# Scales stored as 16 rows, and a rewritten first stretch, in a LayerNorm + S4 + int4 SwiGLU kernel

## What is computed

```
xn = layernorm(u)                                   # over the 1024 channels, no weights
K  = S4 convolution kernel of length 1024 (64 states, from Lambda, p, q, Vc, Ct, B, step)
y1 = irfft(rfft(xn, 2048) * rfft(K, 2048))[..., :1024] + D * xn
Wg, Wu [2752, 1024], Wd [1024, 2752] = (int4 word - zero) * scale, one scale and zero per 64 inputs
h  = silu(xn @ Wg.T) * (xn @ Wu.T)
out = u + y1 + h @ Wd.T
```

## Time and profile before

| | |
|---|---|
| runs (median, lowest to highest) | 1475.91 us, 1475.70 to 1476.86, n = 3 |
| profiled execution | 1472.47 us, span 1470.6 us |
| mean granted TensorE clock | 0.968 |
| busy: TensorE matmul | 1337.2 us, 91% |
| busy: VectorE, GpSimd, ScalarE | 962.1, 678.0, 462.3 us |
| unit 0, unit 2, unit 4 and the down projection begin | 70.7, 164.4, 211.9, about 1001 us |

### The profile page before, as it was taken

One profiled execution on the slowest core, in us unless ns is written; L12 is line 12 of the kernel. 1 busy time (PEld: TensorE's weight loads), 2 busy tenths in 40 slices (PEclk: granted clock), 3 DMA queues, 4 the chain that ended last, 5 costly groups with the idle time before them and its releaser, 6 DMA issues.

```text
span 1470.6 us, 17062 instructions
## 1 busy us (share of the span) xinstructions
PE 1337.2 (91%) x6301; PEld 632.9 (43%) x6301; DVE 962.1 (65%) x1038; ACT 462.3 (31%) x825; POOL 678.0 (46%) x483
## 2 busy tenths in 40 slices
PE   1557798999999999999999999778999999999998
PEld 1533343444443444444444444333454444444444
DVE  3854478999989898999898988624243341432341
ACT  2643335454444544544444444221000000000000
POOL 3643458777777686787979797430000000000000
PEclk9877999999999999999999999998999999999999
DMA  6301144444444444454444443599636336335331
GB/s 178 89 29 70 38 136 148 153 131 165 138 161 147 161 139 154 132 170 139 164 141 165 141 146 120 190 406 316 229 97 224 109 105 213 108 106 197 125 94 57
DMA packets 164358, 218.09 MB, mean 148 GB/s; under 512 B 41394, under 2 KB 121908, under 8 KB 162356
## 3 DMA queue, kind: packets, MB, share of 16 engines
q1 hardware_dynamic: 163412, 202.78, 42.5%
q10 hardware_dynamic: 864, 14.22, 2.3%
HBM read 139.64 MB, written 77.34 MB: 148 GB/s over the span
## 4 chain that ended last, share of the span: by engine, by line
PE 39%; DVE 5%; DMA 4%; POOL 4%; SPq 2%; issue 2%; ACT 1%; ACTq 0%; DVEq 0%
PE px L1381 15%; PE pz L1381 8%; PE pv L1408 5%; PE px L1293 4%; PE py L1381 4%; DMA sz<-in_sz_up 2%; PE pz L1293 2%; POOL wo L660 2%; DVE wf L1466 1%; POOL hs L679 1%; DMA kshift<-kpad 1%; DMA w_d<-ds 1%; POOL ds L669 1%; DVE wf L1464 1%; SPq L568 1%
## 5 line engine op out<-in xcount | busy, mean ns | idle before, releaser
L1293 PE MATMUL px<-xo,wo 128*128 128x512 f16 x2016 | 477.0, 391 | 31.9 <-ACT u L936 19.3
L1293 PEld LDWEIGHTS px<-xo,wo 128*128 128x128 f16 x2016 | 200.7, 101 | 284.4 <-issue 43.5
L660 POOL TENSOR_TENSOR wo<-wf,wo 128x512 f16<-128x512 f32 x147 | 233.5, 1598 | 85.1 <-ACT wo L882 84.7
L679 POOL TENSOR_TENSOR hs<-hf,hs 128x512 f16<-128x512 f32 x154 | 212.3, 1384 | 118.0 <-ACT hs L917 117.8
L1293 PE MATMUL pz<-xo,wo 128*128 128x512 f16 x1008 | 232.6, 381 | 0.0
L1381 PE MATMUL px<-wd,hr 128*128 128x512 f16 x1056 | 232.3, 379 | 0.0
L1381 PEld LDWEIGHTS px<-wd,hr 128*128 128x128 f16 x1056 | 102.2, 98 | 118.7
L1293 PEld LDWEIGHTS pz<-xo,wo 128*128 128x128 f16 x1008 | 99.0, 98 | 119.3 <-issue 2.2
L917 ACT ACTIVATE hs<-hf 128x512 f16<-128x512 f32 x154 | 94.4, 621 | 90.7 <-DVE hf L1556 45.1
L1913 DVE SCALAR_TENSOR_TENSOR acc<-px,acc 128x512 f32<-128x512 f32 x32 | 22.1, 691 | 153.0 <-PE px L1381 125.5
L669 POOL TENSOR_TENSOR ds<-wf,ds 128x512 f16<-128x512 f32 x73 | 113.0, 1547 | 10.8 <-ACT ds L903 10.8
(11 more groups left out here) (217 smaller groups left out, 1417.3 us busy)
## 6 DMA issues: line engine op xcount, KB each, us to landing
h_d<-hs SPq DMA_DIRECT2D x154, 256.0 KB, 4.6
hr<-h_d SPq DMA_DIRECT2D x56, 704.0 KB, 4.3
w_d<-ds SPq DMA_DIRECT2D x73, 256.0 KB, 3.9
wd<-w_d ACTq DMA_DIRECT2D x4, 2816.0 KB, 15.2
sz<-in_sz_gate SPq DMA_DIRECT2D x21, 512.0 KB
sz<-in_sz_up SPq DMA_DIRECT2D x21, 512.0 KB
sz<-in_sz_down SPq DMA_DIRECT2D x20, 512.0 KB
xc_d<-xo SPq DMA_DIRECT2D x8, 1024.0 KB, 10.9
```

Of the source, the lines that this page charges most:

```text
L660: pool.tensor_tensor(w_dest(t, j, 1), w_place_of(j), w_dest(t, j, 0), ALU.subtract).then_inc(wlo_done, 1)
L679: pool.tensor_tensor(hs[:, j, :, 1, :], h_place_of(p, j), hs[:, j, :, 0, :], ALU.subtract)\
L1293: done = pe.matmul(bank[:, :], wo[t % 2][:, j, wp, k * P:(k + 1) * P], xo[p][:, j, xp, k, :], start=(j in (0, 3) and k == 0 and wp == 0 an ...
```

## The change

Two parts.

**Scales.** The host repeats the rows, so that a slab's scales have 16 rows, each read by 8 partitions. The bytes that reach SBUF are the same. In the short slabs the source has one row for 2 partitions in place of one for 32.

**Head.** The 28 transposes of the first half go round all eight banks, those of the second half round five, two or five (HEAD_BANK). The order of the seven blocks of a group is A11, A12, A22, S1, S3, S2, S4 (X_ORDER). All eight groups have buffers of their own, so no load of a group waits; sum S3 overwrites block A21 in place, and the second half has two sets of three sum buffers. SyncE loads all eight groups before the slabs of tile 1. Behind the products of units 0 and 1 stand 2, 3, 1, 1, 1, 1, 3 and 1, 1, 1, 1, 1, 1, 10 transposes (BESIDE). The lists of VectorE, ScalarE and GpSimd until unit 2 are written anew.

```
--- before.py
+++ after.py
+X_ORDER = (A11, A12, A22, S1, S3, S2, S4)
+HEAD_BANK = [("v0", "v1", "x1", "y1", "z1", "x0", "y0", "z0")[(n + 1) % 8] for n in range(28)] + \
+            ["v0", "v1", "x1", "y1", "z1"] * 2 + ["v0", "v1"] * 2 + \
+            ["v0", "v1", "y0", "z0", "x0"] * 2 + ["v0", "v1"] * 2
+def head_bank_free(n):
+    return max([m + 1 for m in range(n) if HEAD_BANK[m] == HEAD_BANK[n]], default=0)
...
+BESIDE = [(28, 30), (30, 33), (33, 34), (34, 35), (35, 36), (36, 37), (37, 40),
+          (40, 41), (41, 42), (42, 43), (43, 44), (44, 45), (45, 46), (46, 56)]
...
-        sum_first = [at(f"xs{q}", [P, 4, SB], f32, X0 + (88 + 8 * q) * K1) for q in range(3)]
-        x_second = [at(f"xb{q}", [P, 2, H], f32, H0 + (20 + 8 * q) * K1) for q in range(2)]
+        sum_first = [at(f"xs{q}", [P, 3, SB], f32, X0 + (88 + 6 * q) * K1) for q in range(4)]
+        x_second = [at(f"xb{q}", [P, 2, H], f32, (H0 + 12 * K1, H0 + 28 * K1, H0 + 20 * K1, W0 + 8 * K1)[q]) for q in range(4)]
...
             def load_x(q):
                 b = 8 * (q // 4) + q % 4
-                if q >= 6:
-                    sp.wait_ge(xt_done, 7 * (q - 1))
...
-                             scales[:, None, :].broadcast_to((4, 32, 1024))).then_inc(slab_in[slot], 16)
+                             scales[:, None, :].broadcast_to((16, 8, 1024))).then_inc(slab_in[slot], 16)
...
-                    z = sz_tail[h, row // 32:(row + n) // 32, :]
+                    z = sz_tail[h, row // 2:(row + n) // 2, :]
...
             load_x(0)
+            load_x(1)
             load_gate(0)
-            load_x(1)
+            load_x(2)
             load_up(0)
-            load_x(2)
-            load_x(3)
+            for q in range(3, 8):
+                load_x(q)
             load_gate(1)
             load_up(1)
...
             load_gate(2)
-            sp.wait_ge(xlo_done, 56)
             load_up(2)
...
             def products(n, t, p, j):
                 if n == 0:
-                    pe.wait_ge(xlo_done, 22 + j)
+                    pe.wait_ge(xlo_done, max(22 + X_POS[j], head_banks_free(("x0", "y0", "z0"), 28)))
+                if n == 1 and j == 0:
+                    pe.wait_ge(xlo_done, head_banks_free(("x1", "y1", "z1"), 42))
...
-            for q in range(4):
-                for j in range(7):
-                    x_transposes(q, j)
+            for b in range(28):
+                x_transposes(b)
             for n in range(2):
                 for i, j in enumerate(TURN):
                     products(n, n, 0, j)
-                    b = 7 * n + i
-                    x_transposes(4 + 2 * b // 7, 2 * b % 7)
-                    x_transposes(4 + (2 * b + 1) // 7, (2 * b + 1) % 7)
+                    for b in range(*BESIDE[7 * n + i]):
+                        x_transposes(b)
...
+    zg, zu, zd, sz_v = (np.repeat(t, 4, axis=-2) for t in (zg, zu, zd, sz_v))
+    tzd = np.repeat(tzd, 16, axis=-2)
```

More of the change, by code:

```diff
@@ L249, in s4_plus_int4_swiglu @@
         xc_d = nc.dram_tensor("xc_d", [2, 2, P, 2, 2, KH, SB], f16, kind="Internal").ap()
-        x_in = [sem(f"x_in{i}") for i in range(6)]
+        x_in = [sem(f"x_in{i}") for i in range(8)]
         slab_in = [sem(f"slab_in{i}") for i in range(2)]
@@ L988, in _ @@
             act.wait_ge(below_done, 1)
+            normalize(0)
             gate_nibble(0)
-            normalize(0)
             normalize(1)
+            x_high(0)
             up_nibble(0)
+            for b in range(1, 4):
+                x_high(b)
+            normalize(2)
+            x_high(4)
             w_high(0, B11)
+            x_high(5)
             w_high(0, B21)
-            for j in range(7):
-                x_high(0, j)
-            normalize(2)
-            w_high(0, B22)
+            for b in range(6, 9):
+                x_high(b)
@@ L999, in _ @@
+            normalize(3)
+            for b in range(9, 12):
+                x_high(b)
+            normalize(4)
+            normalize(5)
+            x_high(12)
+            w_high(0, B22)
+            for b in range(13, 15):
+                x_high(b)
+            normalize(7)
+            for b in range(15, 25):
+                x_high(b)
+            normalize(6)
+            x_high(25)
             w_high(0, T1)
+            x_high(26)
+            snap_s1(0)
+            x_high(27)
             w_high(0, T3)
-            for j in range(7):
-                x_high(1, j)
@@ L1003, in _ @@
-            normalize(3)
+            x_high(28)
             w_high(0, T2)
+            x_high(29)
             w_high(0, T4)
-            for j in range(7):
-                x_high(2, j)
-            for j in range(7):
-                x_high(3, j)
-            normalize(4)
+            x_high(30)
+            snap_s5(0)
+            x_high(31)
             gate_nibble(1)
-            snap_s1(0)
+            x_high(32)
+            up_nibble(1)
+            snap_u2(0)
+            x_high(33)
@@ L1014, in _ @@
             w_high(1, B11)
             w_high(1, B21)
-            for j in range(2):
-                x_high(4, j)
-            normalize(5)
-            up_nibble(1)
-            snap_s5(0)
-            for j in range(2, 4):
-                x_high(4, j)
-            snap_u2(0)
-            for j in range(4, 6):
-                x_high(4, j)
+            x_high(34)
             snap_u3(0)
-            x_high(4, 6)
+            w_high(1, B22)
             silu_first(0)
-            w_high(1, B22)
@@ L1030, in _ @@
             w_high(1, T1)
+            x_high(35)
             w_high(1, T3)
-            for j in range(0, 2):
-                x_high(5, j)
+            x_high(36)
             w_high(1, T2)
+            silu_second(0)
+            x_high(37)
             w_high(1, T4)
-            for j in range(2, 4):
-                x_high(5, j)
-            silu_second(0)
-            normalize(6)
-            for j in range(4, 7):
-                x_high(5, j)
+            for b in range(38, 40):
+                x_high(b)
@@ L1043, in _ @@
             snap_s1(1)
-            for j in range(0, 2):
-                x_high(6, j)
-            normalize(7)
+            x_high(40)
             snap_s5(1)
-            for j in range(2, 4):
-                x_high(6, j)
+            x_high(41)
             snap_u2(1)
-            for j in range(4, 7):
-                x_high(6, j)
+            for b in range(42, 44):
+                x_high(b)
             snap_u3(1)
+            x_high(44)
             silu_first(1)
-            for j in range(7):
-                x_high(7, j)
+            x_high(45)
@@ L1058, in _ @@
             silu_second(1)
+            for b in range(46, 56):
+                x_high(b)
             down_nibble(0, 0)
@@ L1451, in x_stats, with x_low @@
                     .then_inc(stat_done, 1)
-            def x_low(q, j):
-                n = 7 * q + j
+            def x_low(n):
+                q, j = n // 7, X_ORDER[n % 7]
                 dve.wait_ge(xhi_done, n + 1)
@@ L1781, in _ @@
             h_first(0, 0, 0)
+            x_low(35)
             t_sum(1, T4)
[L1783 to L1785 removed]
+            for b in range(36, 40):
+                x_low(b)
             h_second(0, 0, 0)
[L1788 to L1796 removed]
+            for b in range(40, 45):
+                x_low(b)
             c12(1)
             h_first(1, 1, 0)
[L1799 to L1800 removed]
+            x_low(45)
             h_second(1, 1, 0)
+            for b in range(46, 56):
+                x_low(b)
             h_s3(0, 0)
```

218 lines of the change are left out of this document (121 added, 97 removed).

## The result

The changed kernel takes 1408.81 us (median of 4 runs, 1407.06 to 1409.71) against 1475.81 (1473.37 to 1476.86) on the same chip: a ratio of 0.9547, with an interval of 0.9530 to 0.9563. The forecast was 1425 with a range of 1410 to 1447. The profiled execution is 1407.06 us, its span 1405.2, so 65.4 us of span are to be found.

The account below looks back on a forecast made before the run. TensorE was busy 91% of the span, the head bound by engine-to-engine waits. Savings of 39 (head) + 3 + 4 + 5 (scales) = 51 us took 1472.5 to 1421.5; the median lies 3.4 higher, so 1425, range 1410 to 1447.

Parts of the forecast that it names:

- Unit 0 at 57.5: Start of unit 0: VectorE's and GpSimd's lists end together at 57.5 us against 70.73, 13 us saved.
- The full SyncE list costs nothing: it is covered by VectorE: Loads ahead of unit 0: VectorE's list reaches the groups later than they land, but for group 2, about 1 us.
- "14.0 us" for the first sum: GpSimd's first sum, ahead of unit 0, starts at 14.0 us after ScalarE's `normalize(0)`, and not at 22.8.
- The rule on the shared port: Ahead of unit 0: four wide slab instructions each hold up a GpSimd sum; its list 4 us longer, result 1428.
- Units 0 and 1, 68 us: From unit 0 to unit 2: 63 us at full clock plus about 5 for a clock of 0.9.
- The clock as a rival (1457): Rival: the clock stays low in units 0 and 1, at 1.2 GHz throughout, giving 1457 us; chance 0.12.
- Scales, 3 us at the stall beside unit 4: At 220.80 us, scales landing earlier take 3 us off TensorE's gap of 5.43.
- Scales in the groups, 4 us: In nine groups of four units, earlier scales save 0.3 to 0.6 us per group, 4 us in all.
- Scales at the short slabs, 5 us: At the short slabs, the down weights' store goes at once with the scales spread out, saving 5 us.
- The scales stay on four engines: Rival: 16-row scales still use four engines, so only the head counts: 1437 us; chance 0.11.
- A new wait replaces the bank's: Rival: late low parts make each of TensorE's first transposes of unit 1 wait: 1438 us; chance 0.11.
- Clogging: Rival: scale packets clog all sixteen engines, slabs land later if a packet takes over 1.1 us: 1542 us; chance 0.04.

## Why the prediction came out as it did

The step that failed is the price of units 0 and 1: 68 us worked out, 58.5 measured. It had 6 us of waits for weight parts that did not come and 5 us for a low clock of which about 1 came. The second is the price of the scales behind unit 2: 12 us in the sum, 17.5 measured. These 15 us, less 0.5 for unit 0, are the gap between the 51 us forecast and the 65.4 us of span found. A third error does not show in the total: what starts unit 0 early was credited to the head alone. By its own steps:

- **Unit 0 at 57.5.** It was 58.06. The number was right and its account was not, so this hit is in part luck. The loads were put at 350 GB/s throughout, which already takes the scales as spread over sixteen engines, yet the 13 us were booked under the head's order and the scales were given nothing there. With the old scales the same head starts unit 0 at 73.55. The wrong sentence is "The full SyncE list costs nothing: it is covered by VectorE". It is true of the changed kernel, where VectorE is busy for 34.6 of 35 us, and only because of the scales. The row that tells it (17.6 us of VectorE waiting for token groups, in two waits) stands in the view of waits of the kernel before; I had read only ScalarE's wait until 18.45.
- **"14.0 us" for the first sum.** It began at 14.18. GpSimd's first low part began at 55.73, where 55.25 was worked out.
- **The rule on the shared port.** The two sums beside the second slab's wide instructions took 2.24 and 2.25 us against 1.28 just before, and VectorE's took 2.17; beside the first slab one more sum took 2.25 us, at 21.09:

```profile
38.09 1.28 POOL L682 TENSOR_TENSOR xt<-xb 128x512 f32<-128x512 f32 x1 [0.38 <-ACT xb L893]
...
40.73 2.24 POOL L682 TENSOR_TENSOR xb<-xb 128x512 f32<-128x512 f32 x1
42.94 2.25 POOL L682 TENSOR_TENSOR xs<-xa,xs 128x512 f32<-128x512 f32 x1
```

  So each held the other up by 0.9 to 1.0 us. This agrees with the rule that the prediction took from the page "SBUF — State Buffer" (section "Who interferes with whom") of the Trainium skill. Three sums were held up, 2.9 us together, which the forecast left out; and GpSimd stood idle for 2.9 us from 14.18 to 55.73, where about 4 of waits were counted. So the list ended on time in part by luck.
- **Units 0 and 1, 68 us.** They took 58.5. The work was 52.8 us for the 51.8 worked out; the waits were 5.7 and not 11.5, since the second and third product did not wait for weight parts (GpSimd made the first three low parts from 55.73 to 59.59, while TensorE was at the first product until 60.65); the wait ahead of unit 1 was 3.9 for 4.5 and the last transposes 1.7 for 1. The 5 us for a clock of 0.9 were not there: it was 0.97, and the extra of a product at the lower level, 1.7 us behind the 3.93 us wait ahead of unit 1, is inside the 52.8. These 9.5 us, and the 5.5 too few for the scales behind unit 2 (below), put the time out of the range.
- **The clock as a rival (1457).** It did not happen in units 0 and 1. Ahead of unit 0 the clock was low, 0.55 from 22 to 57 us, but there VectorE's list was full (34.59 of 35 us), and TensorE stood 2.5 to 5.2 us for low parts ahead of six of its transposes, so slower transposes cost nothing that shows.
- **Scales, 3 us at the stall beside unit 4.** Measured 3.1 (5.43 to 2.35).
- **Scales in the groups, 4 us.** With the stall it is 9 to 10 us, where 7 was counted: 9 as the remainder of the runs, 10.0 as 17.7 us behind unit 2 (1306.4 to 1288.7) less 7.7 for the short slabs by the spans. Between 240 and 860 us TensorE waited 8.7 us for ScalarE's steps (`u` and `py`) with the old scales in the new head and 2.1 us with the new ones, and between 600 and 860 us no wait is left. The size per group was too low, and the places were right.
- **Scales at the short slabs, 5 us.** It is 7.5 by the run that puts them back. TensorE's two waits there fall from 6.4 and 5.0 us to one of 5.6, which is 5.8. The rest stands in no wait; a product at the lower clock behind each wait would make it up, but that was not separated.
- **"The scales stay on four engines", 1437.** Not what happened, but measured as a kernel of its own: 1440.9. "A new wait replaces the bank's": no, though the 3.9 us ahead of unit 1 are of that kind. "Clogging": the median packet took 206 ns with sixteen engines at work, far from the 1.1 us that were needed.

The parts, in place of 39 + 12: the head 35 (with the old scales), then the scales 32, of which half lay in the head. In the other order they are 28 for the scales and 40 for the head: the parts do not have one price each.

## What to carry to other kernels

When a transfer runs on few of the DMA engines, its price is not only its own landing but that of all that is queued behind it: look for waits on *other* loads near its issue, and expect most where the queue is full. In this kernel two of 62 slabs carried half of what the scales gave, and behind unit 2 a slower landing (8 rows) cost nothing that could be told. Two parts of a change that meet in one stretch can't be priced apart by places in a timeline; one run without each part settles it. Last, a wait in an in-order list can belong to the instruction ahead: one line moved in ScalarE's list gave about 6 us.

## What the runs showed of the hardware that I had not expected

- With 4, 8 and 16 DMA engines at work on a slab of scales the traces show 96, 120 and 300 GB/s, and the median of a 4 KB packet that is read by many partitions rose from 159 ns to 221 and 206. Twice the engines gave a quarter more in that stretch.
- A wait of TensorE can cost more than its length: behind 4.06 us the next product took 4.27 us, without the wait 2.59.
- The view's granted clock can mislead where the trace has no record of it. The kernel with one line moved in unit 2 has the same program as the changed one until then. Its row of 22 to 57 us has the same busy time and says 1.00 where the changed kernel's says 0.55:

```profile
22.00:57.00 35.00, 16.18 (x84) 13.78 (x83) 34.59 (x66) 21.54 (x33) 32.50 (x32) 1.00 0.42 141
```

  But the transposes ran alike, first the changed kernel's, then the other's:

```profile
48.36 1.10 PE L1331 MATMUL pz<-ident,xa 128*128 128x128 f32 x4 [2.46 <-DVE xo L1517]
...
54.90 0.64 PE L1331 MATMUL pv<-ident,xa 128*128 128x128 f32 x4
```

```profile
48.36 1.10 PE L1331 MATMUL pz<-ident,xa 128*128 128x128 f32 x4 [2.46 <-DVE xo L1517]
...
54.84 0.64 PE L1331 MATMUL pv<-ident,xa 128*128 128x128 f32 x4
```

  The first clock record of that trace is at 53.3 us, where the level rises to 1.00, and the transposes turn from 1.06 to 0.64 us there. So the two executions ran at the same pace, and the 1.00 ahead of the first record is no measurement. The length of a known instruction is the surer sign.
